# Which row of DRAM each partition holds, in a kernel of group norm, displacement and blur that streams 403 MB

## What is computed

```python
def _gn(v, G=32, eps=1e-5):            # groups of 12 channels, per image
    g = v.reshape(B_, G, C_ // G, H_, W_)
    m = jnp.mean(g, axis=(2, 3, 4), keepdims=True)
    s = jnp.var(g, axis=(2, 3, 4), keepdims=True)
    return ((g - m) / jnp.sqrt(s + eps)).reshape(v.shape)

# conv: 48 positions of 8 channels each; a position has one displacement
out = _displace(inp, off_round.astype(jnp.int32))   # whole pixels, zeros shifted in
kern = jnp.exp(-(dx * dx + dy * dy) / (2.0 * SIGMA ** 2))   # 3 x 3, per position
kern = kern / jnp.sum(kern, axis=(1, 2), keepdims=True)
out = depthwise_3x3(out, kern)

x = x + conv(_gn(x), L0_conv_offset)
```

## Time and profile before

| | before |
|---|---|
| median of 3 runs | 971.57 us (970.53 to 972.0) |
| the profiled execution | 970.2 us |
| its span, first to last instruction | 968.4 us |
| VectorE busy | 870.7 us (90%) |
| ScalarE busy | 714.2 us (74%) |
| GpSimd busy | 337.3 us (35%) |
| TensorE busy | 201.4 us (21%) |
| moved by DMA | 403.48 MB, mean 417 GB/s |

### The profile page before, as it was taken

The page is one execution under the profiler, slowest core; times in us unless marked ns, Lnnn a source line. Parts: engine busy times, 40 slices in busy tenths (PEclk is TensorE's granted clock), DMA queues, the critical chain, the costliest instruction groups (busy, mean ns, idle before and its releaser), DMA issues.

```text
span 968.4 us, 3636 instructions
## 1 busy us (share of the span) xinstructions
PE 201.4 (21%) x896; PEld 195.9 (20%) x896; DVE 870.7 (90%) x940; ACT 714.2 (74%) x412; POOL 337.3 (35%) x196
## 2 busy tenths in 40 slices
PE   0331312212122121222202212212122122211220
PEld 0331312212122121222202212212122122210220
DVE  5489899999999999899989999999999979669991
ACT  3898959777597777878677776877868787777640
POOL 4022452633524432232325354252623413124320
DMA  8999999999999999999999999999999999999997
GB/s 354 425 408 427 423 418 420 420 422 415 397 430 420 400 428 429 422 417 430 418 425 418 419 408 430 416 415 418 406 432 415 427 428 430 423 427 425 410 432 336
DMA packets 28233, 403.48 MB, mean 417 GB/s; under 512 B 3506, under 2 KB 3506, under 8 KB 3634
## 3 DMA queue, kind: packets, MB, share of 16 engines
q0 software_dynamic: 27648, 402.67, 99.3%
q1 hardware_dynamic: 562, 0.57, 0.2%
HBM read 201.90 MB, written 201.33 MB: 416 GB/s over the span
## 4 chain that ended last, share of the span: by engine, by line
DVE 50%; DMA 35%; issue 5%; ACT 5%; POOL 3%; PE 0%; ACTq 0%; DVEq 0%; POOLq 0%
DMA out<-tiles,row_of 28%; DVE tiles L438 17%; DVE rowblur L413 9%; DVE tiles L440 9%; DVE rowblur L418 9%; DMA tiles<-x,row_of 7%; DVE normed L397 5%; ACT unread L243 4%; POOL tiles L184 2%; ACT unread L247 1%; DVE scale L352 0%; PE var_ps L217 0%; DVE shift L355 0%; DVE var_p L342 0%; DVE apart L336 0%
## 5 line engine op out<-in xcount | busy, mean ns | idle before, releaser
L243 ACT ACTIVATE unread<-tiles 128x4096 uint8<-128x4096 f32 x94 | 339.9, 3616 | 143.3 <-DMA tiles<-x,row_of 142.7
L247 ACT ACTIVATE unread<-tiles,nmean_p 128x4096 uint8<-128x4096 f32 x94 | 348.7, 3709 | 3.0
L184 POOL DMA_INDIRECT tiles<-x,row_of x96 | 162.0, 1687 | 488.7 <-DMA out<-tiles,row_of 483.6
L438 DVE SCALAR_TENSOR_TENSOR tiles<-rowblur,ratio,tiles 128x735 f32<-128x735 f32 (+24 forms) x192 | 300.0, 1562 | 4.6
L189 POOL DMA_INDIRECT out<-tiles,row_of x96 | 175.1, 1824 | 123.5 <-DVE tiles L438 101.0
L217 PE MATMUL mean_ps<-nmean_p,mask 128*128 128x1 f32 x448 | 100.7, 353 | 533.3 <-ACT unread L243 505.8
L217 PEld LDWEIGHTS mean_ps<-nmean_p,mask 128*128 128x128 f32 x448 | 98.0, 330 | 535.9 <-ACT unread L243 508.4
L413 DVE SCALAR_TENSOR_TENSOR rowblur<-normed,ratio 128x784 f32<-128x784 f32 (+14 forms) x96 | 152.3, 1586 | 3.4
L440 DVE TENSOR_TENSOR tiles<-rowblur,tiles 128x784 f32<-128x784 f32 (+14 forms) x96 | 146.5, 1526 | 3.3
L418 DVE SCALAR_TENSOR_TENSOR rowblur<-normed,ratio,rowblur 128x752 f32<-128x752 f32 (+14 forms) x96 | 145.4, 1515 | 3.4
L217 PE MATMUL var_ps<-var_p,mask 128*128 128x1 f32 x448 | 100.7, 353 | 199.3 <-DVE var_p L342 199.3
(11 more groups left out here) (34 smaller groups left out, 25.5 us busy)
## 6 DMA issues: line engine op xcount, KB each, us to landing
tiles<-x,row_of POOLq DMA_INDIRECT x96, 14.7
out<-tiles,row_of POOLq DMA_INDIRECT x96, 17.4
mask<-masks SPq DMA_DIRECT2D x1, 448.0 KB, 3.6
row_of<-rows SPq DMA_DIRECT2D x1, 48.0 KB, 1.7
offs<-offset SPq DMA_DIRECT2D x1, 48.0 KB
plan_sb<-planned SPq DMA_DIRECT2D x1, 0.4 KB
offs_p<-offset SPq DMA_DIRECT2D x1, 0.4 KB
steps_sb<-steps SPq DMA_DIRECT2D x1, 12.0 KB
```

The costliest lines, as they stand in the source:

```text
L184: pool.indirect_dma_start(tiles[:, n % SLOTS, :], None, x_rows, bass.IndirectOffsetOnAxis(ap=row_of[:, n:n + 1], axis=0)).then_inc(loaded[ ...
L243: nc.scalar.activation(unread[:], tiles[:, n % SLOTS, :], ACT.Identity, scale=-1.0 / HW, accum_out=nmean_p[:, i % 2, j:j + 1]).then_inc(nm ...
L247: nc.scalar.activation(unread[:], tiles[:, n % SLOTS, :], ACT.Square, bias=nmean_p[:, i % 2, j:j + 1], accum_out=m2_p[:, i % 2, j:j + 1]). ...
L438: ins = nc.vector.scalar_tensor_tensor(y, t, ratio[:, (tap + 1) // 2, p, 1:2], y, ALU.mult, ALU.add)
```

## The change

In `image_of_partition` the returned arrays are other ones. The text of the change calls `p // 64 * 8 + p // 4 % 8` the engine (0 to 15) and `p // 32 % 2 * 4 + p % 4` the step (0 to 7). Before, in these terms and with engine = 8h + c, a partition held image 2 * step + h, channel c. After, it holds image 8h + c (the engine's number) and channel (step + engine) mod 8. So the eight partitions that have one engine number held one channel of eight images, and hold the eight channels of one image after, begun at channel engine mod 8 and wrapped around.

```diff
 def image_of_partition():
 
     p = np.arange(128)
-    return 2 * (p // 32 % 2 * 4 + p % 4) + p // 64, p // 4 % CH
+    engine, step = p // 64 * 8 + p // 4 % 8, p // 32 % 2 * 4 + p % 4
+    return engine, (step + engine) % CH
```

## The result

The changed kernel takes 984.13 us, the median of four runs between 983.66 and 984.95, against 971.79 us for the kernel before in the same comparison: a ratio of 1.0121 with a 95% interval of 1.0097 to 1.0145. The forecast of 971.6 us was 12.5 us too low; the time lies inside the range of 955 to 992 us, but outside the forecast's own range of 969.7 to 973.5 us. The profiled execution has a span of 982.4 us, 14.0 us more than before.

What follows compares the result with a forecast made beforehand. The prediction took the queue of loads and stores through 16 DMA engines as the bound: 968.4 us span + 0 for addresses + 1.8 outside the span = 970.2, plus 1.4 to the median = 971.6 us; range 955 to 992 us.

Steps and rivals of the forecast that it cites:

- The bound: Whole kernel: time is that of 192 transfers of 2 MiB through 16 DMA engines, with a start and an end.
- Instruction packets: Load intervals: 17 of 83 hold an instruction-queue packet and carry 11.3 of 23.8 us of disturbances; packets the same after.
- I take 0: New DRAM row addresses in loads and stores: forecast to change the time by 0 us.
- the ceiling: Transfer path: 9.72 us for a load and a store, 431.5 GB/s, a hard limit for loads alone and among stores.
- the bounds of -29.1 and +46 us: Address term: all disturbances and end skew gone, or every interval as slow as the slowest slice, 397 GB/s.
- Slower by drift: Transfers: engines a row apart meet on one channel and delay rows; 974 to 1005 us, centre near 985; chance 0.26.
- the faster rival: Transfers: disturbances were in DRAM and part or all of 12.5 us goes; centre 959 us; chance 0.28.
- The last sentence of the prediction: Wrong at its root if the mode goes under 9.70, or loads alone stay at 433 GB/s and the rest slows.
- Slower by the pairs: Transfers: engines e and e+8, now 48 MiB apart, queue at the same memory part; up to 1018 us; chance 0.09.
- Its sign, loads alone at the start below 433 GB/s: Start of the kernel: if the 48 MiB pairs cost, loads alone fall below 433 GB/s and the mode moves.

Runs made afterwards that it cites:

- jump_and_walk: Changed kernel, but engines walk over the channels and move to another image at each row, 16 images at a time; 977.31 us, ratio 1.0071 to the kernel before.
- image_turns: Changed kernel with images moved round the engines by 5 from one unit of three tiles to the next; 982.17 us, ratio 1.0117 to the kernel before.
- no_start: Changed kernel without the rotation: every engine begins at channel 0 of its image; 991.26 us, ratio 1.0207 to the kernel before.
- walk_two_images: Kernel before, but each engine walks over the channels, on the same 2 x 8 rows at each step; 971.01 us, ratio 1.0002.
- near_pairs: Changed kernel, but engine 8h + c holds image 2c + h, so engines e and e+8 are 6 MiB apart; 986.02 us, ratio 1.018 to the kernel before.
- far_pairs: Kernel before, but engine 8h + c at step s holds image s + 8h, so engines e and e+8 are 48 MiB apart; 970.33 us, ratio 1.0007.
- the third phase: Part of the kernels without computing: 96 loads and 96 stores in turn; 83 intervals took 808.8 us with rows of before, 828.4 with those of after.
- phases_before: Kernel before without computing: 96 loads alone, then 96 stores alone, then both in turn; 1908.99 us, against 1926.05 us with the rows of after.

## Why the prediction went as it did

**The bound: right.** The time is that of the queue of transfers; VectorE's busy time moved by 0.2 us and the 14.0 us are all in how long the transfers take. The most frequent interval is 9.71 to 9.73 us in every layout, and the packets' 611 ns are nearly the same statement (16 rows of an engine are 9.78 us). The prediction called 397 GB/s the slowest of the page's 40 slices; the first and the last, with the start and the end in them, are slower.

**Instruction packets: right in number, the share not shown.** They are as many as before, and their intervals carry 11.9 instead of 11.3 us. That the two agree is partly luck: in the other layouts the intervals with such a packet carry from 5.3 us (jump_and_walk) to 14.5 us (image_turns). The rest of the disturbances was the part that addresses could move, and it did: 12.5 to 25.4 us.

**The step that failed: "I take 0".** I set the term of the addresses to 0 because most intervals sat on the ceiling and because before and after touch the same 8 places modulo 128 KiB at each step. The first was true and says nothing on the others: a few rows in a hundred are slow, and their number grew from 1065 to 1706 while the median stayed. The second took the place modulo 128 KiB for the thing that counts. It does count (no_start: 0.9%), but so do how many images are under way and how long an engine stays in one, together 1.2% here, and the term had nothing for them. The term measured 14.0 us in the span, well between the bounds of -29.1 and +46 us that the rows gave. That the time fell inside the range of 955 to 992 us is luck as far as the mechanism goes: the range reached that high for a rival whose cause the runs don't bear out.

**The rivals.** Slower by drift had the best numbers, a centre near 985 us, the mode kept and more outliers, and the wrong cause: walk_two_images has the meeting engines and ratio 1.0002. The prediction's own argument from the earlier trace rows, that loads alone at the start ran at 433 GB/s with the jumps of before, was used against the faster rival and for one ceiling for loads alone and loads among stores. It holds for loads alone, and that is its weakness: the start shows only about 1 us of the cost (0.2 us of slow rows per engine before, 1.1 after), which for the rest needs stores beside the loads. The last sentence of the prediction named this as the way to be wrong at the root, and priced it only by the worst slice. Slower by the pairs fell twice, in near_pairs and far_pairs: with the pairs 48 MiB apart, and an engine's jump 6 instead of 12 MiB, the ratio is 1.0007. Its sign, loads alone at the start below 433 GB/s, did come for three slices, but it comes in near_pairs too, with three slices of 352 to 379 GB/s, so it isn't a sign of the pairs. Faster had the right quantity (the disturbances without an instruction packet) and the wrong sign. That partitions belong to engines as the change says still has no row of its own; the layouts were built on that map, and that their times follow what it says of an engine's path fits it.

**What stays open.** Why loads and stores disturb each other more when the engines are spread over more images and stay in them. The runs rule out as the cause by itself: the distance of the pairs, the walk over the channels, the neighbouring row and an engine tied to an image; and, by one execution, the same image on both sides. The number of turns is doubtful. They don't show what the two directions contend for, nor why without computing the loss dies down. Nor do they separate "images at a time" from "rows in one image" fully: an engine that stays in one image for eight rows means sixteen images, and the two layouts with 16 images and no stay differ from the change by 0.5 to 0.8%, with intervals that nearly touch.

## What to carry to other kernels

A kernel that is bound by loads and stores together can't be judged by its loads: a layout of addresses that is free for loads alone and for stores alone cost 1.2% where they alternate. Without computing it cost 20 us, two thirds of it in the first 16 pairs of transfers after the start, so a short test without computing shows it but doesn't give its size for a long kernel. In this kernel the engines did best in two images at a time, on neighbouring rows, each leaving its image at every row; giving each engine a region of its own was worse, and there different offsets at the start gave back 0.9%. And when most intervals sit on a ceiling, look at the tail: after the change 93% of the rows still took at most 650 ns (96% before), and the extra time of the others, 14 us per engine more than before, is the whole loss.

## What the runs showed beyond that

The kernel before has 21.3 us of slow rows per engine, yet the same loads and stores in turn without computing have little: the third phase runs at 430 GB/s, a mean interval of 808.8 / 83 = 9.74 us, against 10.007 us in the kernel. So of the 23.8 us of disturbances that I had put down to instruction packets and DRAM, some 83 x (10.007 - 9.74) = 22 us come with computing beside the transfers, with the moments at which it lets stores go, or with its instruction packets (23 in the kernel, 3 in all of phases_before). Which of the three wasn't tried. It may also be why the layouts differ by 20 us without computing and by 13.5 us with it, since with it part of the disturbances is there in either layout; no run shows that.

Stores alone are a little slower than loads alone, 455.4 / 91 = 5.00 us against 445.8 / 91 = 4.90 us for a transfer of 2 MiB, and the two in turn by before's rows are faster than either, 9.74 / 2 = 4.87 us. The first two phases have four transfers under way and the third up to ten, so direction and depth aren't told apart.
